# A four-layer Mamba stack ahead of twelve attention steps: the first unit prepared in an order of its own over three PSUM pairs, its weights loaded before the stream, one signal for each half of dt, and softplus written with four VectorE instructions

## The reference

```python
p = silu(prepend_cond @ pre_w1) @ pre_w2      # 64 tokens put ahead of the 512
h = concatenate([p, x], axis=1)               # 576 tokens
for l in range(4):
    h = h + mamba_block(rmsnorm(h, norm_w[l]), ...)
h = rmsnorm(h, final_norm_w)[:, 64:, :]

def mamba_block(x, ...):
    xz = x @ ip_w.T                           # 1024 columns
    xi, z = split(xz, 2)
    xi = silu(conv(xi))                       # 4 taps along the tokens, per channel
    xdbl = xi @ xp_w.T                        # 16 + 16 + 16 columns
    dt, Bm, Cm = split(xdbl, [16, 32])
    dt = softplus(dt @ dtp_w.T + dtp_b)       # 512 channels
    A = -exp(A_log)
    h_t = exp(dt * A) * h_(t-1) + dt * Bm * xi   # 16 states per channel, one after another in t
    y = sum over the states of h_t * Cm, + xi * Dp
    return (y * silu(z)) @ op_w.T
```

## Time and profile before

| | us |
|---|---|
| median of 3 runs (lowest, highest) | 5450.53 (5450.38, 5451.68) |
| the profiled execution | 5452.39 |
| its span | 5450.6 |
| DVE busy in the span | 3964.5 (73%) |
| PE busy | 4907.3 (90%) |
| ACT busy | 2298.4 (42%) |
| POOL busy | 2608.0 (48%) |
| start of the first scan (L638) | 117.12 |
| end of the last scan | 2444.80 |

### The profile page before, as it was taken

One profiled execution on the slowest core, in us unless ns is written; L12 is line 12 of the kernel. 1 busy time (PEld: TensorE's weight loads), 2 busy tenths in 40 slices (PEclk: granted clock), 3 DMA queues, 4 the chain that ended last, 5 costly groups with the idle time before them and its releaser, 6 DMA issues.

```text
span 5450.6 us, 53833 instructions
## 1 busy us (share of the span) xinstructions
PE 4907.3 (90%) x18976; PEld 2672.2 (49%) x18976; DVE 3964.5 (73%) x3886; ACT 2298.4 (42%) x4022; POOL 2608.0 (48%) x1334
## 2 busy tenths in 40 slices
PE   5889888888888888876999889999999999999999
PEld 3455555555555555533555444555544445555444
DVE  2999999999999999993777662766656246665641
ACT  3555554555555555533434333433333233333321
POOL 0555555555555555563777311766610036665000
PEclk8999999999999999987999999999999999999999
DMA  2334444434443444331000110000010000001000
GB/s 79 138 138 146 148 146 142 145 141 145 143 142 140 145 141 146 134 130 36 1 1 1 39 39 0 1 1 1 1 47 32 8 1 1 1 1 47 1 1 16
DMA packets 94440, 376.70 MB, mean 69 GB/s; under 512 B 13024, under 2 KB 14432, under 8 KB 91232
## 3 DMA queue, kind: packets, MB, share of 16 engines
q1 hardware_dynamic: 94176, 373.26, 19.5%
HBM read 369.94 MB, written 3.28 MB: 68 GB/s over the span
## 4 chain that ended last, share of the span: by engine, by line
PE 45%; DVE 5%; ACT 1%; issue 1%; POOL 1%; DMA 0%; SPq 0%; DVEq 0%; ACTq 0%
PE PS L1061 6%; PE PS L1085 6%; PE PS L1071 6%; PE PS L1040 6%; PE PS L1247 5%; PE PS L1258 3%; PE PS L1049 3%; PE PS L1095 3%; PE PS L1207 2%; PE PS L1171 1%; PE PS L1159 1%; DVE PA L1589 1%; DVE CST L1587 1%; POOL PA L1004 1%; PE PS L1027 1%
## 5 line engine op out<-in xcount | busy, mean ns | idle before, releaser
L571 POOL TENSOR_TENSOR UH<-UH,BC 128x1152 f32<-128x1152 f32 x512 | 1343.8, 2625 | 1094.8 <-DVE U L630 1094.8
L1004 POOL TENSOR_SCALAR PA<-PA,INV 128x512 f32<-128x512 f32 x768 | 1189.9, 1567 | 600.9 <-DVE INV L1503 600.8
L356 PE MATMUL Y<-UH,ident_sb 128*128 128x512 f32 (+1 forms) x3072 | 1173.8, 527 | 223.7 <-POOL UH L571 169.0
L638 DVE TENSOR_TENSOR_SCAN UH<-DA,U 128x1152 f32<-128x1152 f32 x512 | 1307.2, 2553 | 22.9 <-ACT DA L515 5.5
L356 PEld LDWEIGHTS Y<-UH,ident_sb 128*128 128x128 f32 x3072 | 591.9, 203 | 843.3 <-issue 571.0
L515 ACT ACTIVATE DA<-DT,NEGA 128x575 f32<-128x575 f32 x1024 | 718.7, 763 | 329.3 <-DVEq L622 234.9
L1318 ACT ACTIVATE PA<-PS,NMX 128x512 f32<-128x512 f32 x768 | 518.9, 683 | 725.7 <-DVE NMX L1497 554.8
L630 DVE TENSOR_TENSOR U<-DTX,BC 128x1152 f32<-128x1152 f32 x512 | 701.1, 1369 | 49.5 <-DVEq L622 4.2
L1512 DVE COPY VP<-PS 128x512 f32<-128x512 f32 x768 | 495.1, 686 | 281.2 <-PE PS L1071 259.1
L1497 DVE TENSOR_REDUCE NMX<-PS 128x2 f32<-128x1024 f32 x384 | 452.5, 1219 | 50.1 <-PE PS L1061 49.9
L1071 PEld LDWEIGHTS PS<-ident_sb,PA 128*128 128x128 f32 x3072 | 352.5, 142 | 241.3 <-issue 195.2
(11 more groups left out here) (133 smaller groups left out, 5347.7 us busy)
## 6 DMA issues: line engine op xcount, KB each, us to landing
BC<-bc_rows SPq DMA_DIRECT2D x512, 576.0 KB, 3.7
WA<-mamba_a SPq DMA_DIRECT2D x16, 1421.0 KB, 7.4
W<-pair_w SPq DMA_DIRECT2D x6, 3072.0 KB, 10.4
WB<-mamba_b SPq DMA_DIRECT2D x16, 514.0 KB, 5.1
VP<-ff_w SPq DMA_DIRECT2D x2, 3072.0 KB
WO<-out_w SPq DMA_DIRECT2D x4, 1024.0 KB
stream<-x_t SPq DMA_DIRECT2D x2, 1024.0 KB, 6.9
VP<-ff_w SPq DMA_DIRECT2D x2, 1024.0 KB
```

What stands on the lines that cost most here:

```text
L356: mm = pe.matmul(Y[:, a:b], IDENT[:, :], UH[:, SLOT[j], a:b], start=(s == 0), stop=(s == DS - 1), skip_group_check=True)
L571: pool.tensor_tensor(h, h, BC[:, j % NBB, 1, :].unsqueeze(1).broadcast_to([P, HK, T]), ALU.mult).then_inc(s_hc, 1)
L638: dve.tensor_tensor_scan(UH[:, SLOT[j], :], DA[:, j % NDA, :], U[:, 0:HC], 0.0, ALU.mult, ALU.add).then_inc(s_scan, 1)
L1004: pool.tensor_scalar(PR[:, n % 3, j, :], PR[:, n % 3, j, :], INV[:, n % 4, j:j + 1], None, ALU.mult).then_inc(s_ps, 1)
```

## The change

The head: the identity has no block of its own any more. SP issues `pre_w`, the context, `ONES`, the identity, `DV` (one DMA), `WA`, and only then the stream, `FIN` and `WB`. PE waits for `pre_w` and the context alone. ACT builds the diagonal matrices right after the two silu of the prepended tokens.

Window -1: PE, ACT and DVE follow a table `FIRST` instead of `PREP_AT`. Its third number says which of three PSUM pairs a step takes: `PAIR`, or the first 1024 columns of `Y` or `U`, which hold nothing yet. A step waits only for the last reader of its own pair. The order differs too (`xz` 6 behind `dt` 1, `xz` 7 last). The table load ahead of `silu_x` moves ahead of the read of `cv` 3, and the decay rates `NEGA` are made behind `dt` 0. DVE does only the first half of unit 0's softplus in window -1 and the second in slots 1 and 2 of window 0.

The signal: `s_dt` is counted up after the first half of dt, `s_dt2` after the second; `drive` and `decay` wait for `s_dt2` in slot 16.

Softplus: ACT takes the relu and the square of the small-w term (L525, L526 of the new kernel, into `DTX`) and DVE is left with four instructions a half instead of five. `silu_z` moves from slot 30 of the window that prepares a unit to slot 1 of the window that scans it.

```diff
-SILU_X, SILU_Z = 21, 30
...
-
-def window_uses(prep, end):
-
+FIRST = [("ms", 0, 0), ("xz", 0, 1), ("xz", 1, 2), ("xz", 2, 0), ("xz", 3, 1), ("cv", 0, 2), ("cv", 1, 0), ("cv", 2, 1),
...
+
+def first_free(i):
...
+        EDGC = sb("EDGC", [P, 2])
...
-        pair = PAIR[:, :, 0:HT]
+        PAIRS = [PAIR[:, :, :]] + [ps[:, 0:1024].rearrange("p (a n) -> p a n", a=2) for ps in (Y, U)]
...
+        s_dt2 = step("s_dt2")
...
+                sp.dma_start(ZS[:, 0:2 * 2 * D], pre_w).then_inc(s_prew, 16)
+                sp.dma_start(XS[:, 0:2 * NB * NPRE], ctx_t).then_inc(s_prew, 16)
                 sp.dma_start(ONES[:, :], ones).then_inc(s_const, 16)
+                sp.dma_start(IDENT[:, :], ident).then_inc(s_ident, 16)
+                sp.dma_start(DV[:, :, :], wb[:, :, B_D:B_D + KI].rearrange("l p c -> p l c")).then_inc(s_dvec, 16)
+                sp.dma_start(WA[:, :], wa[0, :, :]).then_inc(s_wa, 16)
+                for k in range(KD):
+                    sp.dma_start(hT[:, :, :].rearrange("p k (b t) -> p k b t", t=T)[:, k, :, NPRE:T],
+                                 x_t[:, k, :, :]).then_inc(s_h, 16)
                 sp.dma_start(FIN[:, :], fin_norm).then_inc(s_const, 16)
-                for l in range(NL):
-                    sp.dma_start(DV[:, l, :], wb[l, :, B_D:B_D + KI]).then_inc(s_dvec, 16)
-                sp.dma_start(hT[:, :, :].rearrange("p k (b t) -> p k b t", t=T)[:, 0, :, NPRE:T],
-                             x_t[:, 0, :, :]).then_inc(s_h, 16)
-                sp.dma_start(hT[:, :, :].rearrange("p k (b t) -> p k b t", t=T)[:, 1, :, NPRE:T],
-                             x_t[:, 1, :, :]).then_inc(s_h, 16)
-                sp.dma_start(XS[:, 0:2 * NB * NPRE], ctx_t).then_inc(s_h, 16)
-                sp.dma_start(ZS[:, 0:2 * 2 * D], pre_w).then_inc(s_h, 16)
...
+                        sp.wait_ge(s_sp, START + n * (KI // KD))
...
-                            load_a(0)
...
-                pe.wait_ge(s_const, 32)
-                pe.wait_ge(s_h, 64)
+                pe.wait_ge(s_prew, 32)
...
+                pe.wait_ge(s_const, 32)
+                pe.wait_ge(s_ident, 16)
+                pe.wait_ge(s_h, 32)
...
-                        if scan or end or done[0]:
+                        if scan or end:
                             pe.wait_ge(s_free, START + base + done[0])
+                        elif first_free(done[0]):
+                            pe.wait_ge(s_free, START + first_free(done[0]))
+                        elif FIRST[done[0]][2] == 1:
+                            pe.wait_ge(s_pact, START + KD)
+                        elif FIRST[done[0]][2] == 2:
+                            pe.wait_ge(s_pact, START + 2 * KD)
                         done[0] += 1
 
                     def halves(out_rows, lhs, rhs, start, stop):
+                        to = PAIRS[0 if scan or end else FIRST[done[0] - 1][2]]
                         for a in range(2):
-                            mm = pe.matmul(PAIR[0:out_rows, a, 0:HT], lhs, rhs(a), start=start, stop=stop)
+                            mm = pe.matmul(to[0:out_rows, a, 0:HT], lhs, rhs(a), start=start, stop=stop)
...
+                    if not scan and prep:
+                        for kind, i, _ in FIRST:
+                            prep_step(kind, i)
+                        return
...
+                act.wait_ge(s_wa, 16)
+                act.wait_ge(s_ident, 16)
+                act.wait_ge(s_dvec, 16)
+                diagonals(0, 0)
+                diagonals(0, 1)
...
-                    k0 = 8
+                    k0 = 10
...
+                    def pair():
+                        return PAIRS[0 if scan or end else FIRST[at[0]][2]][:, :, 0:HT]
...
+                            own(act.activation(E[:, i, :].rearrange("p (a n) -> p a n", a=2), pair(), ACT.Abs, bias=bias))
                             act.sem_inc(s_free, 1)
                             if i % 2:
                                 two = slice(i - 1, i + 1)
                                 own(act.activation(E[:, two, :], E[:, two, :], ACT.Exp, scale=-1.0))
-                                act.activation(LG[:, two, :], E[:, two, :], ACT.Ln, bias=SHRC[:, 0:1],
-                                               scale=SHRINK).then_inc(s_sp, 1)
-                            if i == KI - 1:
+                                act.activation(LG[:, two, :], E[:, two, :], ACT.Ln, bias=SHRC[:, 0:1], scale=SHRINK)
+                                sq = DTX[:, bass.ds(off + (i - 1) * T, KD * T)].rearrange("p (c t) -> p c t", c=KD)
+                                own(act.activation(sq, E[:, two, :], ACT.Relu, bias=EDGC[:, 0:1], scale=-1.0))
+                                act.activation(sq, sq, ACT.Square, bias=EDGC[:, 1:2], scale=-HALF_ROOT).then_inc(s_sp, 1)
+                            if i == (KI - 1 if scan else 0):
                                 own(act.activation(ALOG[:, :], WA[:, A_LOG:A_COLS], ACT.Exp))
                                 act.activation(NEGA[:, bass.ds(npar * (KI * DS), KI * DS)], ALOG[:, :], ACT.Copy,
                                                scale=-1.0).then_inc(s_nega, 1)
...
-                        act.preload_act_table_set("silu_and_others")
+                        if scan:
+                            act.preload_act_table_set("silu_and_others")
                         act.activation(XS[:, bass.ds(off, KI * T)], XS[:, bass.ds(off, KI * T)], ACT.Silu).then_inc(s_xs, 1)
                         act.preload_act_table_set("natural_log_exp_and_others")
 
                     def silu_z():
                         act.preload_act_table_set("silu_and_others")
-                        act.activation(ZS[:, bass.ds(off, KI * T)], ZS[:, bass.ds(off, KI * T)], ACT.Silu).then_inc(s_zs, 1)
+                        act.activation(ZS[:, bass.ds(par * (KI * T), KI * T)], ZS[:, bass.ds(par * (KI * T), KI * T)],
+                                       ACT.Silu).then_inc(s_zs, 1)
...
                     def decay(j):
                         h, s = j // DS, j % DS
+                        if j == DS:
+                            act.wait_ge(s_dt2, START + n + 1)
                         if j >= NDA or end:
...
+                    if not scan and prep:
+                        squares()
+                        for kind, i, _ in FIRST:
+                            if (kind, i) == ("cv", KI - 1):
+                                act.preload_act_table_set("silu_and_others")
+                            prep_read(kind, i)
+                            if (kind, i) == ("cv", KI - 1):
+                                silu_x()
+                        assert step[0] == k0, step
+                        return
...
                         if prep and j == SILU_X:
                             silu_x()
-                        if prep and j == SILU_Z:
+                        if scan and j == SILU_Z:
                             silu_z()
                         if scan and j + 2 < NJ:
                             decay(j + 2)
                         if prep and j in (2, 3) and nxt % NB == 0:
-                            diagonals(j - 2)
...
-                    def softplus(k, part_two):
+                    def softplus(of, k, part_two):
                         if not part_two:
-                            dve.wait_ge(s_sp, START + nxt * (KI // KD) + k // KD + 1)
-                        o = off + k * T
+                            dve.wait_ge(s_sp, START + of * (KI // KD) + k // KD + 1)
+                        o = of % 2 * (KI * T) + k * T
                         dt = DT[:, bass.ds(o, KD * T)].rearrange("p (c t) -> p c t", c=KD)
 
-                        e, ln, part = E[:, k:k + KD, :], LG[:, k:k + KD, :], E[:, k:k + KD, :]
+                        e, ln = E[:, k:k + KD, :], LG[:, k:k + KD, :]
                         if not part_two:
-                            own(dve.tensor_scalar(part, e, EDGE, -0.5, ALU.min, ALU.mult))
-                            own(dve.scalar_tensor_tensor(out=part, in0=part, scalar=1.0, in1=part, op0=ALU.add, op1=ALU.mult))
+                            own(dve.scalar_tensor_tensor(out=dt, in0=ln, scalar=0.0, in1=dt, op0=ALU.max, op1=ALU.add))
+                            own(dve.scalar_tensor_tensor(out=dt, in0=e, scalar=EDGE, in1=dt, op0=ALU.min, op1=ALU.add))
                         else:
-                            own(dve.scalar_tensor_tensor(out=dt, in0=part, scalar=-2.0, in1=dt, op0=ALU.mult, op1=ALU.add))
-                            own(dve.scalar_tensor_tensor(out=dt, in0=ln, scalar=0.0, in1=dt, op0=ALU.max, op1=ALU.add))
+                            own(dve.tensor_tensor(DT[:, bass.ds(o, KD * T)], DT[:, bass.ds(o, KD * T)],
+                                                  DTX[:, bass.ds(o, KD * T)], ALU.subtract))
                             own(dve.tensor_tensor(DTX[:, bass.ds(o, KD * T)], DT[:, bass.ds(o, KD * T)],
                                                   XS[:, bass.ds(o, KD * T)], ALU.mult))
-                            if k:
```

(36 more changed lines are left out.)

62 lines of the change are left out of this document (37 added, 25 removed).

## The result

The changed kernel takes 5410.84 us (median of 4 runs, 5407.05 to 5411.92), the kernel before 5450.45 (median of 4, 5447.68 to 5451.68): ratio 0.9927, 95% interval 0.9910 to 0.9944. It is 40 us faster, where 58 were forecast, and 5410.8 lies above the range of 5380 to 5408. The profiled execution took 5411.92 us, its span 5410.1: 40.5 us less than before.

The account below looks back on a forecast made before the run. Bound by DVE's instructions between first and last scan, and before that by one chain from DMAs over PE and ACT. 5452.4 - 26.4 - 24.3 - 3.6 - 3.7 = 5394.4, predicted median 5392.5 us, range 5380 to 5408.

Parts of the forecast that it names:

- Head and window -1: Before the first scan: scan at 84.9 against 117.12, 32.2 us gained, net 26.4 after DVE's half softplus in window 0.
- The second rival: PE stays cold in window -1, its warm steps some 20 us longer: 5412; chance 5%.
- The softplus: DVE's preparations under scans: 0.81 us less a half, 30 halves, 24.3 us gained; bounds 0 and 41.7.
- The gate: DVE's wait for PE at the gates, 3.9 us in all, should go through earlier squares: 3.7 us gained.
- The signal: The 0.24 us that drive(0) waited for DVE's own signal goes, 15 times: 3.6 us gained, or 0.
- ACT at slot 3 and slot 27: ACT in time by 3 us at slot 3, 4.1 at slot 27; rival: 0.6 to 2 late for scan 3, 7%.
- The slower rival: PE's queue in slots 26 to 31: sums behind steps awaiting ACT come late for scans, 5452 and above; chance 3%.
- is the sum of DVE's instructions: First to last scan: DVE busy 2253.9 of 2327.7 us, so each instruction taken off DVE is gained.

Follow-up runs that it names:

- experiment 12: The changed kernel with gate in slot 1, xz 4 in slot 19, signal on the instruction, and softplus in five instructions again: 5408.30 us.
- experiment 3: The changed kernel with ten matmuls, whose results nobody reads, added on PE ahead of the slot-2 gate: 5399.65 us.
- experiments 6 and 8: The changed kernel with decays waiting for the second half's signal and silu_z in slot 30: 5408.28 us; the changed kernel with softplus in five instructions: 5426.59 us.
- experiment 10: The changed kernel with DVE's signal of each half given by the last softplus instruction itself: 5399.69 us.
- Experiment 7: The changed kernel with decays of units 1 to 15 waiting for the second half's signal, silu_z staying in slot 1: 5413.82 us.
- the gate in slot 1: The changed kernel with DVE's gate for the last half of the unit before moved from slot 2 to slot 1: 5399.53 us.

## Why the prediction was wrong

- **Head and window -1.** Right: 30.9 us against 32.2. The parts are right within about 2 us, and the forecast of 84.9 lies inside the spread of 83.0 to 86.5. The second rival (PE cold in window -1) did not happen; the convolutions ran at 4.05.
- **The softplus.** Right. 18.5 us net with the half in window 0 was forecast. Counted from the start of each of its instructions to the start of the next, without the idle time behind the signal, it took 18.4 us less of the stretch; experiment 12 gives 0.84 us a half.
- **The gate.** This step failed: "The wait for PE at the gate, 3.9 us in all, should go", with 3.7 us gained. It was 7.1 us lost, 10.8 off. I read the group's row, which mixes the gates of slots 2 and 17, as the one at the window's end, because that one has PE's late mean of squares ahead of it. In the timeline it never waited. The gate that waits, in slot 17, hangs on PE's chain of some 64 us from the gate of slot 2 on, which starts only there, so an earlier mean of squares gains nothing for it. What it met instead is a lower clock at the start of that chain, 0.64 in the mean against 0.78, which DVE pays at slot 17; filling the hole of 7 us brought the waits from 11.0 to 1.7 us (experiment 3). The early signal, which made the hole, and the softplus of four instructions each have a part: without the one the waits are 6.1, without the other 5.6 (experiments 6 and 8). How the second acts is open.
- **The signal.** "The 0.24 us that `drive(0)` waited for DVE's own signal goes, 15 times: 3.6" failed too. It was not the wait for `s_dt` but the wait for the instruction and the increment behind it (experiment 10), and the change has two a unit: 3.1 us lost, 6.7 off. I had written that it could stay and gave 0 as the bound; doubling was not in it.
- These two are 17.5 us, as much as the difference between 58 and 40.5. What else is off, 1.3 us at the head among it, is small and cancels. That the two sums agree so closely is luck.
- **ACT at slot 3 and slot 27.** Right: no scan waited for a decay in the units. Experiment 7 shows that the slack in slot 3 is as thin as taken: 0.4 to 1.3 us late in 11 units where 0.6 to 2 was written for all fifteen.
- **The slower rival** was near the truth in its place, PE's queue, and wrong in its slots: it looked at slots 26 to 31, where PE idles, and not at 2 to 17, where it does not. The statement that the stretch "is the sum of DVE's instructions" is what hid it; the earlier trace rows with 2002.8 us of PE was the warning that I explained away.

## What to carry over

When a wait of a few tenths of a us recurs, find which instance of the line has it before you say what removes it: a group's row adds up places with different chains. Where two engines need nearly the same time between two meeting points, look at each stretch between them for the one with no idle time; work taken off the other gains only until then. And work moved ahead of a wait leaves a hole behind it. On TensorE the matmuls behind the hole may then run at a lower clock, so look at the granted clock there, over all rounds and not in one, and move the wait with the work, as the gate in slot 1 does.

## What the hardware showed

An instruction's wait for itself followed by a separate increment cost DVE 0.21 to 0.24 us of idle time, with the increment on the instruction none; in 31 places that made the stretch 8.6 us shorter, although the waits at slot 17 grew by 1.9. The 0.03 us between two instructions that wait for each other stayed. The clock behind the same 7 us hole was not the same in every unit of the changed kernel: 0.54, 0.76, 0.61, 0.53, 0.75, 0.63 and so on in turn; why it goes in turn was not tried.
